# Two layers of attention and routed experts on one core: the first layer's experts by unordered pairs, gathers without clears between them

## What is computed

```python
xn = layernorm(x)
s = causal_attention(xn @ W + b)                 # layer 1, one head of 128
h = layernorm(xn) * ln_g + ln_b
abel = gelu(h @ aw1 + ab1) @ aw2 + ab2           # dense part, 128 -> 512 -> 128
top2 of 6 logits(h), softmax over the two        # K = 2, E = 6
moe = sum_e w_e * (gelu(h @ ew1[e] + eb1[e]) @ ew2[e] + eb2[e])   # 128 -> 256 -> 128
nonabel = moe @ expm(gens[0]) @ ... @ expm(gens[3])
gate = sigmoid([abel, nonabel] @ gc_w + gc_b)
x = x + s * silu(xn + abel * (1 - gate) + nonabel * gate)
xn = layernorm(x)
x = x + attention_8_heads(xn) * silu(top1_of_8_experts(xn))       # layer 2, 128 -> 512 -> 128
```

## Time and profile before

| what | us |
|---|---|
| median of 3 runs (lowest, highest) | 713.91 (711.11, 715.43) |
| the profiled execution | 718.61 |
| its span | 716.9 |
| busy in it: TensorE, DVE, ACT, POOL | 626.8, 496.5, 415.2, 447.6 |

### The profile page before, as it was taken

How to read it: one execution, slowest core, us unless ns; L and a number is a source line. 1 busy time by engine, 2 the same in 40 slices (tenths; PEclk the granted TensorE clock), 3 DMA queues, 4 the chain that set the end, 5 groups by cost and what they waited for, 6 DMA issues and landing times.

```text
span 716.9 us, 19568 instructions
## 1 busy us (share of the span) xinstructions
PE 626.8 (87%) x6221; PEld 443.8 (62%) x6222; DVE 496.5 (69%) x1302; ACT 415.2 (58%) x1144; POOL 447.6 (62%) x663
## 2 busy tenths in 40 slices
PE   4799889786876997896799999995999999999994
PEld 3667767686875865675354555554999845555442
DVE  5678776667665716998488888883444477887884
ACT  2575334443443454776666787773444367878793
POOL 7775888887068869974122476764333258878782
PEclk9999999999999999998999999998999999999997
DMA  8995111144566621110010000001222101111110
GB/s 230 289 301 149 42 45 56 56 113 87 104 114 127 128 56 33 31 24 13 1 32 2 8 32 24 24 28 35 69 70 70 56 21 42 32 32 31 32 46 16
DMA packets 69466, 48.34 MB, mean 67 GB/s; under 512 B 8011, under 2 KB 63750, under 8 KB 69382
## 3 DMA queue, kind: packets, MB, share of 16 engines
q1 hardware_dynamic: 62332, 34.09, 18.4%
q0 software_dynamic: 6144, 12.63, 7.3%
q10 hardware_dynamic: 906, 0.55, 0.3%
HBM read 24.00 MB, written 23.24 MB: 66 GB/s over the span
## 4 chain that ended last, share of the span: by engine, by line
PE 41%; POOL 23%; issue 17%; DVE 8%; DMA 5%; ACT 3%; SPq 1%; DVEq 0%; ACTq 0%; POOLq 0%
PE bank L1746 6%; PE bank L1817 5%; PE bank L1826 5%; POOL vs L1658 5%; POOL pool_xy L1056 5%; PE bank L1012 4%; DMA xg<-x_half 4%; PE bank L1726 3%; POOL xn_all L1634 3%; PE bank L1115 2%; POOL spacer L1051 2%; PE bank L1125 2%; DVE nmx L2058 2%; PE bank L579 2%; PE bank L1105 1%
## 5 line engine op out<-in xcount | busy, mean ns | idle before, releaser
L1891 ACT ACTIVATE pb<-bank,nmx 128x512 f32<-128x512 f32 x256 | 173.5, 691 | 65.5 <-DVE nmx L2058 62.6
L2058 DVE TENSOR_REDUCE nmx<-bank 128x2 f32<-128x1024 f32 x128 | 155.1, 1215 | 13.3 <-PE bank L1746 11.8
L1227 ACT ACTIVATE turns<-bank,cols 128x128 f32<-128x128 f32 x148 | 46.4, 364 | 65.5 <-PE bank L1115 41.4
L1658 POOL TENSOR_TENSOR vs<-vt_first,rz 128x256 f32<-128x256 f32 x64 | 39.4, 615 | 70.9 <-DVE rz L2034 69.9
L1726 PEld LDWEIGHTS bank<-pb,vs 128*32 128x32 f32 x2048 | 54.5, 110 | 37.6 <-issue 19.4
L1726 PE MATMUL bank<-pb,vs 128*32 128x128 f32 x2048 | 69.6, 275 | 2.0 <-POOL vs L1658 2.0
L382 POOL DMA_INDIRECT x_half<-pool_xy,slot x64 | 62.3, 973 | 10.6 <-issue 10.6
L1746 PE MATMUL bank<-qk 64*128 64x512 f32 x256 | 65.6, 622 | 1.6 <-ACT pb L1891 1.1
L1746 PE MATMUL bank<-qk_first 64*128 64x512 f32 x256 | 64.6, 619 | 2.2 <-ACT pb L1891 1.0
L1658 POOL TENSOR_TENSOR vs<-vt,rz 128x256 f32<-128x256 f32 x64 | 39.2, 615 | 36.5 <-DVE rz L2034 32.1
L1691 POOL COPY xn_all<-w 128x512 f32 x39 | 23.9, 615 | 51.3 <-PE bank L1817 49.2
(11 more groups left out here) (275 smaller groups left out, 1450.6 us busy)
## 6 DMA issues: line engine op xcount, KB each, us to landing
y_half<-ys SPq DMA_DIRECT2D x74, 64.5 KB
x_half<-zero SPq DMA_DIRECT2D x2, 2368.0 KB, 17.6
xg<-x_half SPq DMA_DIRECT2D x74, 64.0 KB
x_sorted<-zero SPq DMA_DIRECT2D x1, 2496.0 KB, 18.5
xn_all<-x_sorted SPq DMA_DIRECT2D x39, 64.0 KB, 1.8
y_sorted<-xn_all SPq DMA_DIRECT2D x39, 64.0 KB, 1.6
x_all<-in_L_attn_x_dram SPq DMA_DIRECT2D x8, 256.0 KB, 6.8
w<-in_L_ffn_W_dram SPq DMA_DIRECT2D x1, 2048.0 KB, 11.9
```

Of the source, the lines that this page charges most:

```text
L1658: pool.tensor_tensor(vs[s][:, :, :], vt[bt % 2][:, n // 2 % TT, :, :].rearrange("p j d -> p (j d)") .unsqueeze(1).broadcast_to([P, 2, D]), ...
L1891: act.activation(pb[s + ab][:, :], psum[score_banks(k) + ab], ACT.Exp, bias=nmx[:, s + ab:s + ab + 1], scale=1.0, accum_out=zz[:, s + ab:s ...
L2058: dve.tensor_reduce(nmx[:, s:s + 2], banks[:, score_banks(k):score_banks(k) + 2, :], AX.X, ALU.max, negate=True).then_inc(n_mx, 1)
```

## The change

A token's two experts form one of 15 unordered pairs. Tokens are sorted by pair over all tokens at once, into 46 blocks of 128 rows; a block runs both experts of its pair. The row in DRAM has 130 columns, with the two weights behind the values. The weighted sum of the two experts and their biases is made in the expert stage on DVE (four operations a block in place of one), so each token has one slot, one scatter and one gather. Scatters start once, after the routing of batch 4. POOL, not DVE, copies the first weights, two copies a block. xg has six buffers, held until the block is done. There is no clear between the gathers, and all gathers stand behind the expert stage: eight, then two before and two after `power` of each batch. `first_part`, `residual` and `gate_scales` go; `mix` makes the whole sum. `next_scores` of TensorE moves behind the first down chunk of the next batch, `next_T` by one chunk. Layer 2's scatters come one per two half steps. New routing tables for pairs (`cls`, `pair_weights`, `block_experts` in batches 5 and 6) stand in place of those of the halves.

```diff
-    NBH = 2 * NTH + E0 - 1
-    NB0 = 2 * NBH
+    NC = E0 * (E0 - 1) // 2
+    NB0 = NT + NC - 1
     DX = D + 1
+    DW = D + 2
+    FIRST_OF = [a * E0 - a * (a + 1) // 2 for a in range(E0)]
...
-        NXG = 4
-        xg0 = [sbe(f"xg0{i}", [P, D]) for i in range(NXG)]
+        NXG = 6
...
             def scatter(g):
-                for slot_w in (slot1, slot2):
...
+                pool.indirect_dma_start(
+                    out=x_pair, out_offset=bass.IndirectOffsetOnAxis(ap=slot0[:, g:g + 1], axis=0),
+                    in_=xh[:, g, :], in_offset=None).then_inc(t_sc0, 16)
+                space()
...
-            for h in range(2):
-                pool.wait_ge(a_sl, h + 1)
-                pool.wait_ge(t_zf[h], 16)
-                for g in range(h * NTH, (h + 1) * NTH):
-                    scatter(g)
+            pool.wait_ge(a_wt, 2)
+            pool.wait_ge(a_sl, 1)
+            pool.wait_ge(t_zf[0], 16)
+            for g in range(NT):
+                scatter(g)
...
+            def ranks():
+                pe.wait_ge(a_mo, 2)
+                pe.wait_ge(t_cst, 18)
+                for bank, w in ((psum[2], tri), (psum[1], ones)):
+                    mm = pe.matmul(bank[:, 0:NC * NT], w[:, :], cls[:, :, :].rearrange("p c t -> p (c t)"),
+                                   start=True, stop=True)
...
+                if bt == ROUTES[1]:
+                    act.wait_ge(a_dmr, 2)
+                    act.activation(th[:, :], dm[:, :], ACT.Exp).then_inc(f_th, 1)
...
+                dve.tensor_tensor(sg[:, half], sn[:, half], mt[:, :], ALU.is_gt)
+                step(dve.tensor_tensor(mo[:, :, :], oh1[:, half, :], oh2[:, half, :], ALU.add))
+                for a in range(E0 - 1):
+                    n = E0 - 1 - a
+                    last = dve.tensor_tensor(cls[:, FIRST_OF[a]:FIRST_OF[a] + n, half],
+                                             mo[:, :, a + 1:E0].rearrange("p t e -> p e t"),
+                                             mo[:, :, a].unsqueeze(1).broadcast_to([P, n, NTH]), ALU.mult)
+                last.then_inc(a_mo, 1)
...
+            def pair_weights():
+                dve.wait_ge(f_th, 1)
+                dve.tensor_scalar(sn[:, :], sg[:, :], -1.0, 1.0, ALU.mult, ALU.add)
+                step(dve.tensor_scalar(w_best[:, :], th[:, :], 1.0, None, ALU.add))
+                step(dve.reciprocal(w_best[:, :], w_best[:, :]))
+                step(dve.tensor_tensor(w_next[:, :], th[:, :], w_best[:, :], ALU.mult))
+                for i, (u, v) in enumerate(((w_best, w_next), (w_next, w_best))):
+                    dve.tensor_tensor(wp[:, :], sg[:, :], u[:, :], ALU.mult)
+                    step(dve.tensor_tensor(wq[:, :], sn[:, :], v[:, :], ALU.mult))
+                    dve.tensor_tensor(xh[:, :, D + i], wp[:, :], wq[:, :], ALU.add).then_inc(a_wt, 1)
+                    dve.wait_ge(a_wt, i + 1)
...
+            def slots():
                 step(dve.tensor_tensor(off0[:, :, :], off0[:, :, :], over_t(beg0[:, :]), ALU.add))
...
+                step(dve.tensor_tensor(offo[:, :, :], off0[:, :, :], cls[:, :, :], ALU.mult))
+                step(dve.tensor_reduce(sl_f[:, :], offo[:, :, :].rearrange("p c t -> p t c"), AX.X, ALU.add))
+                dve.tensor_copy(slot0[:, :], sl_f[:, :]).then_inc(a_sl, 1)
...
@@ -915,8 +962,10 @@
                 if not more:
                     rotated_column()
                 store_turned(2)
...
+            for k in range(NB0):
+                both = expert(k)
+                if k >= NW:
+                    pool.wait_ge(o_up, k - NW + 1)
+                for i in range(2):
+                    pool.tensor_copy(wst0[k % NW][:, i * H0:(i + 1) * H0],
+                                     w_e1[:, bass.ds(both[i], 1), :].rearrange("p a h -> p (a h)")).then_inc(o_w, 1)
...
+                pool.indirect_dma_start(
+                    out=yg0[:, g, :], out_offset=None, in_=y_pair,
+                    in_offset=bass.IndirectOffsetOnAxis(ap=slot0[:, g:g + 1], axis=0)).then_inc(f_yg[g // TT], 16)
...
-            for g in range(4):
-                gather(NTH + g)
-            for bt in range(1, B + 2):
-                first = 4 + (0, 2, 4, 6, 8, 9, 11)[bt - 1] if bt < B else NTH
-                if bt <= B:
-                    residual(bt - 1)
-                if first < NTH:
...
-                if 2 <= bt:
-                    power(bt - 2)
-                if first + 1 < NTH and bt != 5:
-                    gather(NTH + first + 1)
+            for j in range(NY):
+                pool.wait_ge(o_st[j], 16 * ((NB0 - 1 - j) // NY + 1))
+            for g in range(2 * TT):
+                gather(g)
+            for bt in range(2, B + 2):
+                if bt < B:
+                    gather(bt * TT)
+                    gather(bt * TT + 1)
+                power(bt - 2)
+                if bt < B:
+                    gather(bt * TT + 2)
+                    gather(bt * TT + 3)
...
-                pe.wait_ge(o_w, k + 1)
+                pe.wait_ge(o_w, 2 * k + 2)
...
+                for i in range(2):
+                    for c in range(EC):
+                        mm = pe.matmul(psum[MBANK[k % 2]][:, i * DX:(i + 1) * DX],
+                                       hT0[k % NW][:, (i * EC + c) * P:(i * EC + c + 1) * P],
+                                       w_e2[:, bass.ds(both[i] * EC + c, 1), :].rearrange("p a d -> p (a d)"),
+                                       start=(i == 0 and c == 0), stop=(c == EC - 1), skip_group_check=True)
...
-                    pe.wait_ge(f_u, bt - 1)
+                    pe.wait_ge(f_r, bt - 1)
...
-                if n == 2 and bt > 2:
+                if n == 3 and bt > 2:
                     next_T(bt - 3)
                 down(c)
-                if n == 3 and bt > 2:
-                    next_scores(bt - 3)
+                if n == 0 and bt > 3:
+                    next_scores(bt - 4)
+            next_scores(B - 4)
...
+                        ins = act.activation(hT0[k % NW][:, at:at + P], psum[k % 2][:, at:at + P], ACT.Gelu,
+                                             bias=cols[:, bass.ds(both[i] * EC + (ROW_EB1 + c), 1)], scale=1.0)
...
-                if bt:
-                    act.wait_ge(f_u, bt)
-                act.activation(og[:, :], gt[:, :], ACT.Copy, bias=0.5, scale=-0.5).then_inc(f_og, 1)
-                act.activation(gg[:, :], gt[:, :], ACT.Copy, bias=0.5, scale=0.5).then_inc(f_gg, 1)
-
-            def first_part(bt):
-                act.wait_ge(f_og, bt + 1)
...
+                    act.wait_ge(f_r, bt - 1)
+                act.activation(og[bt % 2][:, :], gt[:, :], ACT.Copy, bias=0.5, scale=-0.5)
...
+                if bt:
+                    gate_tanh(bt - 1)
+                gelu(bt * AC + 2)
                 if bt > 1:
                     silu_tanh(bt - 2)
-                if bt:
-                    gate_tanh(bt - 1)
...
+                if bt + 1 < B:
+                    gelu(bt * AC + 4)
...
+            bias_of = lambda e: b2x[:, bass.ds(e, 1), :].rearrange("p a d -> p (a d)")
+            weight_of = lambda k, i: xg0[k % NXG][:, D + i:D + i + 1]
+
+            def first_bias(k):
+                if k >= NY:
+                    dve.wait_ge(o_st[k % NY], 16 * (k // NY))
+                dve.tensor_scalar(ys0[k % NY][:, :], bias_of(expert(k)[0]), weight_of(k, 0), None, ALU.mult).then_inc(o_b1, 1)
+
+            def second_bias(k):
+                dve.wait_ge(o_b1, k + 1)
+                dve.scalar_tensor_tensor(ys0[k % NY][:, :], bias_of(expert(k)[1]), weight_of(k, 1), ys0[k % NY][:, :],
+                                         ALU.mult, ALU.add).then_inc(o_b2, 1)
+
...
+                dve.wait_ge(o_b2, k + 1)
+                dve.scalar_tensor_tensor(ys0[k % NY][:, :], psum[MBANK[k % 2]][:, 0:DX], weight_of(k, 0), ys0[k % NY][:, :],
+                                         ALU.mult, ALU.add).then_inc(o_f1, 1)
+
+            def second_expert(k):
+                dve.wait_ge(o_f1, k + 1)
+                dve.scalar_tensor_tensor(ys0[k % NY][:, :], psum[MBANK[k % 2]][:, DX:2 * DX], weight_of(k, 1), ys0[k % NY][:, :],
+                                         ALU.mult, ALU.add).then_inc(o_y, 1)
+
...
+                dve.wait_ge(f_yg[bt], 16 * TT)
+                if bt:
+                    dve.wait_ge(f_gt, bt)
                 dve.wait_ge(f_dn, (bt + 1) * AC)
...
+                dve.tensor_tensor(gz[:, 0:3], yg0[:, bt * TT:bt * TT + 3, D],
+                                  a[:, 0:3 * DX].rearrange("p (t d) -> p t d", t=3)[:, :, D], ALU.add)
...
+                a, b_ = (psum[i] for i in ABANKS[bt % 2])
+                dve.wait_ge(f_gg, bt + 1)
+                dve.wait_ge(f_xa, bt + 1)
                 for t in range(TT):
-                    y = in_half(bt * TT // NTH, bt * TT + t)
-                    ins = dve.scalar_tensor_tensor(r[:, t, :], y[:, 0, 0:D], gw1[:, t:t + 1], r[:, t, :], ALU.mult, ALU.add)
```

(20 more changed lines are left out.)

303 lines of the change are left out of this document (123 added, 180 removed).

## The result

The changed kernel takes 739.73 us (median of 4 runs, 737.27 to 742.74) where the kernel before takes 714.67 (4 runs, 711.11 to 716.12): a ratio of 1.034 with a 95% interval of 1.029 to 1.039. It is slower, by 25 us; 735 had been forecast. The profiled execution took 737.3 us, its span 735.6. Some executions of any of these kernels are longer than the rest for no reason in the kernel, at a lower granted clock; ratios leave them out.

What follows compares the result with a forecast made beforehand. It took one loop through POOL, DVE and ACT to bound the dense part, and work per block the expert stage. +0.8, +20.7, +4 and -4 make +21.5, on the median 713.9: 735 us, range 712 to 752.

Steps and rivals of the forecast that it cites:

- 1. Start: Before the experts: later scatters, then POOL's bias sums and mq scaling, put the first expert matmul at 155.9, +15.4 us.
- the side remark that attention lengthens to 146 at most: Layer 1 attention: block tables on DVE, twice about 3.3 us, lengthen it to 146 at most, under the scatters.
- 2. Experts: Layer 1 expert stage: 46 blocks at 2.05 us, 99.9 us to the last down matmul; stage -14.7, with the start +0.8.
- rival (c): Expert stage gains nothing: DVE's register loads count, 2.6 us a block, 26 us more, 761 us; chance 0.08.
- Rival (b): Experts gain more: 1.90 us a block, start at 152, warm clock, 720 us; chance 0.08.
- 3. Dense part: Dense part of layer 1: the new order makes loops of 11.4 to 13.0 us through POOL and DVE, +20.7 us.
- the clock: Dense part: TensorE's idle time puts matmuls that DVE waits for at the lower clock level, +4 us.
- Both waits that the forecast named: Dense loop: gate_sums stalls 4.5 us on gathers behind `power`; next_scores waits for scores queued behind a down chunk needing mix.
- The landing: Dense loop: time from a gather's end until its data can be used, taken as 1.0 us.
- a full 8 us: Dense part: clock cost if both groups DVE waits for start cold, 1.6 us in five loops; half was taken.
- Rival (a): Dense loop doesn't close through POOL; TensorE's 8.6 us a batch decides, 709 us; chance 0.16.
- 4. Layer 2: Ahead of layer 2's experts: scatters finish earlier, so TensorE's 7.2 us wait shrinks, -4 us.

Runs made afterwards that it cites:

- pool path: Changed kernel with the last four bias sums and mq's scaling moved behind the weight copies of blocks 6 to 14: 740.86 us, 1.026 of the kernel before.
- start all: Changed kernel with bias sums and mq's scaling behind later weight copies, block tables at their batch's end, no clears between scatters: 772.77 us, 1.069 of the kernel before.
- the experiment's trace: Changed kernel with all four gathers of a batch issued ahead of `power`: 730.11 us, 1.017 of the kernel before.

## Why the prediction was right, step by step

**1. Start, +15.4, measured +16.9.** Scatter start 98.2 in the forecast, measured 99.7; pitch 1.57, measured 1.6 (148.8 to the last from 99.7); sums and mq at 4.93 and 1.52, on the path. The mechanism and its size held. What failed is the side remark that attention lengthens to 146 at most: it ended at 152.7. The block tables were sized well enough (4.4 and 3.6 against "3.3 twice") but taken to be free, and they stand where TensorE waits. It cost nothing in the sum because POOL was later still; once POOL's path is freed, it bounds the start, as the run with the pool path shows.

**2. Experts, 99.9, measured 100.2.** 17 instructions at the pitch of layer 2's block and 2.05 a block: from the first to the last group of down matmuls 163.2 to 256.8 for 45 steps is 2.08. The register loads stayed hidden, so rival (c) is out. Rival (b) is out as well: not 1.90 a block but 2.08, and a start at 157.4, not 152.

**3. Dense part, +20.7 and +4 for the clock, measured +25.5.** (From the last down matmul, T0, to layer 2's first scores 118.4 us against 92.9.) mix(0) was forecast at T0 + 18.8 and ended at T0 + 18.6 (276.2); the last mix at T0 + 105.9 with the clock, measured T0 + 107.3. Both waits that the forecast named are in the chain and both are paid: taking one away gave 12 us, the other 5, both 18. One term was small. The landing was taken as 1.0 and is 1.5 behind the second gather's record (310.1 to 311.7 in one loop), in all some 0.5 a loop. The Trainium skill ("DMA: Bandwidth & Descriptors", Anatomy of one DMA) gives about 2 us of fixed time; here 2.5 pass from the gather's start to DVE, of which its own record holds 0.95. As for the clock, the two groups that DVE waits for lose 1.6 a loop, as worked out, in the loops of 15.0 and 15.1 and some 0.5 in the two of 13.9, together 4: half of 8 came out. That it did is partly luck, since "start all" with the same dense code lost next to nothing there. The loop at the upper clock measured 13.4 where 13.0 was the forecast, and against that the last step, without gathers, was forecast at 8.3 and took 6.6. The prediction also reads a full 8 us out of the Trainium skill's rule ("TensorE: Matmul & The Clock Gate", HAM oscillation), which is for bursts shorter than their waits; by its own numbers (8.6 us of work a batch, some 5 idle) the bursts here are longer, so the condition isn't met, though the clock fell all the same.

Rival (a), that TensorE's 8.6 decides, lost for the reason given against it. But it was nearer than it looked: by the experiment's trace TensorE was only 1 to 2 us behind in each loop, because the idle that the gathers bring on slows TensorE itself.

**4. Layer 2, -4, measured -4.7**, and 5.0 in the run that has it alone. The mechanism is the one forecast: TensorE's wait of 7.2 us ahead of the experts became 1.85.

The sum was +21.5; the medians differ by 25.1. Of the missing 3.6, 1.5 are the start, 0.3 the experts, 0.8 the dense part with its tail; layer 2's start gives back 0.7 and its experts take 0.5 more (77.0 us against 76.5). The last 1.2 are less than the spread of either kernel's runs.

## What to carry to other kernels

An instruction moved behind another on one engine's queue inherits that one's waits. Write down the loop through all engines (here DVE, POOL, the landing, ACT, TensorE and back) before halving its work, since halving the work left it longer. Where an engine idles for 2 or 3 us in each turn of such a loop, look at its clock too, and after each wait removed ask what was 1 us behind it. And test a bundle's parts alone: here leaving out clears gains 0.8% and an earlier end of layer 2's scatters some 5 us, and the order of a dozen lines costs 18.

## What the runs showed of the hardware

A loop of 11.4 to 13.9 us with one TensorE gap of 1.8 to 1.9 us in it ran at a granted clock of 0.84; with the gap filled by useless matmuls it ran at 1.00 and the kernel became 1.1% faster. A gap of 0.94 in a loop of 9.5 left it at 1.00. Loops of one and the same code, with gaps of 1.8 to 4.8, took 13.4 to 15.2 us, the longest where the lower level fell on the matmuls that were waited for. Indirect DMAs back to back on POOL start 1.25 to 1.3 us apart (0.96 and 0.30), with a 0.43 us clear between them 1.57 to 1.6. And there is a combination of such back-to-back scatters and work moved elsewhere in which, by a trace with records missing, ACT and TensorE nearly stand still for some 30 us, and which made the kernel 25 us slower in four of four runs; the cause is open.
